# A two-layer transformer block on one core: a new step order for the first feed-forward, grouped bias products, and stack transposes later in an attention slot

## The reference

```python
# layer 0, attention: 16 heads of 16, causal, then a projection
ctx = softmax(mask(Q K^T) / 4) V          # Q, K, V from x @ W.T
x = LN(x + ctx @ Wp.T + bp)
# layer 0, feed-forward: 8 experts, all computed, 2 of them weighted per token
gates = top-2 of softmax(x @ router_w + router_b), renormalised
h = gelu(x @ expert_w[e] + expert_b[e])   # e = 0..7, 256 wide
x = LN(x + (sum_e gates[e] * h[e]) @ out_w + out_b)
```

## Time and profile before

| | |
|---|---|
| median of 3 runs | 989.48 us (987.34 to 991.6) |
| the profiled execution | 989.61 us, span 987.7 us |
| busy share of the span | PE 89%, DVE 73%, ACT 52%, POOL 39% |
| first attention | to about 262 us |
| first feed-forward | to about 453 us, partly overlapped |
| mean granted TensorE clock | 0.965 of full |

### The profile page before, as it was taken

One profiled execution on the slowest core, in us unless ns is written; L12 is line 12 of the kernel. 1 busy time (PEld: TensorE's weight loads), 2 busy tenths in 40 slices (PEclk: granted clock), 3 DMA queues, 4 the chain that ended last, 5 costly groups with the idle time before them and its releaser, 6 DMA issues.

```text
span 987.7 us, 22438 instructions
## 1 busy us (share of the span) xinstructions
PE 875.0 (89%) x8350; PEld 538.7 (55%) x8457; DVE 717.2 (73%) x1955; ACT 513.9 (52%) x1201; POOL 383.7 (39%) x729
## 2 busy tenths in 40 slices
PE   5887878987579888998999999999999999899996
PEld 2444545443234444335555666766666676577654
DVE  3776766676567877657999888888888888733566
ACT  3566657666224343436666665555555555432542
POOL 3543445444334554442333333332333332300185
PEclk8998989999779999999999999999999999999999
DMA  7323322320000000002676766555555666600011
GB/s 261 101 82 81 67 54 66 89 29 7 2 1 1 1 1 1 1 1 41 121 120 117 112 99 103 96 104 97 95 99 103 98 104 95 119 3 1 1 44 43
DMA packets 210428, 65.64 MB, mean 66 GB/s; under 512 B 203008, under 2 KB 206608, under 8 KB 210192
## 3 DMA queue, kind: packets, MB, share of 16 engines
q1 hardware_dynamic: 210320, 64.19, 33.3%
HBM read 17.92 MB, written 4.19 MB: 22 GB/s over the span
## 4 chain that ended last, share of the span: by engine, by line
PE 53%; DVE 21%; issue 7%; POOL 6%; DMA 6%; ACT 6%; SPq 1%; POOLq 0%; DVEq 0%; ACTq 0%
PE bank L417 12%; PE bank L418 11%; PE bank L416 10%; DMA att<-w_lo 5%; PE bank L760 3%; PE bank L762 3%; PE bank L761 3%; DVE nm L1230 3%; PE bank L543 3%; DVE w_lo L1254 2%; ACT scr L895 2%; DVE scr L1172 2%; ACT att L941 2%; POOL scr L1714 2%; PE bank L464 2%
## 5 line engine op out<-in xcount | busy, mean ns | idle before, releaser
L985 ACT ACTIVATE att<-att,nm 128x512 f32<-128x512 f32 (+3 forms) x256 | 141.5, 553 | 104.1 <-DVE nm L1243 102.7
L416 PE MATMUL bank<-w_hi,scr 128*128 128x256 bf16 (+1 forms) x566 | 169.4, 299 | 6.1 <-DVE scr L1172 3.1
L417 PE MATMUL bank<-w_lo,scr 128*128 128x256 bf16 (+1 forms) x575 | 173.1, 301 | 1.9 <-issue 1.8
L418 PE MATMUL bank<-w_hi,scr 128*128 128x256 bf16 (+1 forms) x572 | 171.9, 301 | 0.1
L895 ACT ACTIVATE scr<-bank 128x256 bf16<-128x256 f32 (+3 forms) x208 | 110.2, 550 | 112.1 <-PE bank L762 43.0
L1230 DVE TENSOR_REDUCE nm<-bank 128x1 f32<-128x512 f32 (+3 forms) x256 | 110.3, 483 | 44.0 <-PE bank L488 44.0
L1243 DVE CUSTOM_DVE_ANT_0 att<-bank,consts 128x512 f32<-128x512 f32 (+3 forms) x256 | 113.4, 483 | 15.0 <-PE bank L418 15.0
L941 ACT ACTIVATE att<-bank 128x512 f32<-128x512 f32 (+1 forms) x192 | 90.9, 528 | 61.3 <-PE bank L527 60.6
L1749 POOL TENSOR_SCALAR wqkv_hi<-att,rr 128x512 bf16<-128x512 f32 (+3 forms) x128 | 66.0, 535 | 140.2 <-DVE rr L1260 140.2
L1172 DVE TENSOR_TENSOR scr<-bank,scr 128x256 bf16<-128x256 f32 (+1 forms) x144 | 75.1, 535 | 48.2 <-ACT scr L895 48.2
L1749 POOL TENSOR_SCALAR w_hi<-att,rr 128x512 bf16<-128x512 f32 (+3 forms) x128 | 66.0, 535 | 104.6 <-DVE rr L1260 104.6
(11 more groups left out here) (177 smaller groups left out, 2107.4 us busy)
## 6 DMA issues: line engine op xcount, KB each, us to landing
scr<-wall_in SPq DMA_DIRECT2D x19, 512.0 KB, 4.7
x_tok<-x_tok_in SPq DMA_DIRECT2D x1, 2048.0 KB, 10.2
v_by_token<-scr SPq DMA_DIRECT2D x16, 128.0 KB, 1.8
scr<-v_by_token SPq DMA_DIRECT2D x16, 128.0 KB, 3.2
scr<-x_t_in SPq DMA_DIRECT2D x3, 512.0 KB, 6.0
out<-x_tok SPq DMA_DIRECT2D x3, 512.0 KB, 2.7
scr<-wqkv_in SPq DMA_DIRECT2D x2, 384.0 KB, 3.4
att<-w_hi SPq DMA_TRANSPOSE x32, 3.3
```

The lines of the kernel that those rows point to most:

```text
L416: pe.matmul(out, l_hi, r_hi, start=start, stop=False, skip_group_check=check)
L417: pe.matmul(out, l_hi, r_lo, start=False, stop=False, skip_group_check=check)
L418: return pe.matmul(out, l_lo, r_hi, start=False, stop=stop, skip_group_check=check)
L985: last = act.activation(at, at, ACT.Exp, bias=nm[:, j % 2, qt:qt + 1], scale=-1.0, accum_out=rs[:, j % 2, qt:qt + 1])
```

## The change

1. `small_weights` runs in slot 18 (`SMALL_SLOT`); the load of the biases stands with the first loads; the pieces are laid out in slot 27 by twelve DMAs, three to each of the partitions 0, 32, 64 and 96, in the place of a used q/k/v weight.
2. The bias products are issued together, for the four pairs of experts, each on its own 32 rows of the array, behind the six products of experts 0.
3. The order of a step changes on all engines, as the diff shows. The join of the two sums moves from the end of step t to step t + 1, cm turn and second product to the end of step t + 1, `joined(t, 2)` and `norm(t, 2)` to step t + 2.
4. In attention, `l0_stack` comes after the context turns (even slots) and after `l0_context(g, 0)` (odd slots).
5. `x_low` of blocks 2 and 3 is POOL's, in slots 7 and 15.

```diff
-TURN_LEADS = (("x1", LEAD), ("x2", -2), ("cm", -1), ("cc", LEAD + 2))
+TURN_LEADS = (("x1", LEAD), ("cc", LEAD + 2), ("cm", -1), ("x2", -2))
 STEPS = range(-LEAD - 2, NT + 2)
 EARLY = range(-LEAD - 2, -2)
 TURNS = [(kind, n + lead) for n in STEPS for kind, lead in TURN_LEADS if 0 <= n + lead < NT]
 DVE_X = 5
-MIX = DVE_X + 1
...
 BIAS_SLOTS = range(27, 31)
+SMALL_SLOT = 18
...
+        eb3 = wqkv_hi[:, 0, 0:512]
...
-        eb3 = scr[0:3, 15360:16384].bitcast(BF16)
...
             sp.dma_start(b1_col[:, :], b1_d).then_inc(ld_b, 16)
+            sp.dma_start(eb_f, eb_d).then_inc(ld_b, 16)
...
-                    sp.wait_ge(ch_done, NCH)
-                    sp.dma_start(eb_f, eb_d).then_inc(ld_b, 16)
-
-            sp.wait_ge(eb_ready, 1)
-            for i in range(3):
-                sp.dma_start(eb3[i:i + 1, :], eb_p[:, i, :]).then_inc(eb_moved, 16)
+                if p == BIAS_SLOTS[0]:
+                    sp.wait_ge(eb_ready, 1)
+                    sp.wait_ge(a["vp"], NT)
+                    for q in range(4):
+                        for i in range(3):
+                            sp.dma_start(eb3[32 * q + i:32 * q + i + 1, :], eb_p[4 * q:4 * q + 4, i, :]
+                                         ).then_inc(eb_moved, 16)
+
...
                     if chunk == 0 and 0 <= p + 1 < NP:
                         l0_row_maxima(p + 1)
+                    if chunk == 1 and j == 0 and 0 <= g - 1 < NT:
+                        l0_context_turns(g - 1)
+                    if chunk == 1 and j == 1 and 0 <= g < NT:
+                        l0_context(g, 0)
                     if chunk == 1 and 0 <= g + 2 < NT:
                         l0_stack(g + 2, j)
-                    if chunk == 1 and j == 0 and 0 <= g - 1 < NT:
-                        l0_context_turns(g - 1)
                     if chunk == 2 and 0 <= g + 3 < NT:
                         (l0_project, l0_values)[j](g + 3)
-                    if chunk >= 1 and j == 1 and 0 <= g < NT:
-                        l0_context(g, chunk - 1)
+                    if chunk == 2 and j == 1 and 0 <= g < NT:
+                        l0_context(g, 1)
                     if (p, chunk) in EARLY_AT:
                         if EARLY_AT[p, chunk] == 0:
                             pe.wait_ge(ch_done, 1)
...
-                hold(pe, m["ge"], 4 * (t - 1) + p + 1)
                 out = bank[4 + p][:, :]
-                pe.matmul(out, ones_b[0:3, :], eb3[:, p * 512:(p + 1) * 512], start=True, stop=False)
+                if p == 0:
+                    hold(pe, m["ge"], 4 * (t - 1) + 1)
                 for k in range(KE):
                     cs = slice(EXPW + k * NX * E + p * 512, EXPW + k * NX * E + (p + 1) * 512)
                     last = mm3(out, tb_hi[t % TB][:, k * P:(k + 1) * P], tb_lo[t % TB][:, k * P:(k + 1) * P],
-                               w_hi[:, cs], w_lo[:, cs], False, k == KE - 1)
+                               w_hi[:, cs], w_lo[:, cs], p == 0 and k == 0, p > 0 and k == KE - 1)
+                if p == 0:
+                    hold(pe, m["ge"], 4 * t)
+                    for q in (1, 2, 3, 0):
+                        rows = slice(32 * q, 32 * q + 3)
+                        last = pe.matmul(bank[4 + q][:, :], ones_b[rows, :], eb3[rows, :], start=(q > 0), stop=(q == 0),
+                                         tile_position=(32 * q, 0))
                 last.then_inc(m["f"], 1)
...
-            pe.wait_ge(eb_moved, 48)
+            pe.wait_ge(eb_moved, 12 * 16)
...
                     l1_project("k", 0)
                 if here:
                     experts(n, 0)
-                if 0 <= n + 4 < NT and (n + 4) % TT == TT - 1:
+                routed = 0 <= n + 4 < NT and (n + 4) % TT == TT - 1
+                if routed:
                     logits((n + 4) // TT)
-                if 0 <= n - 2:
-                    turn_mix("x2", n - 2)
-
-                routed = 0 <= n + 4 < NT and (n + 4) % TT == TT - 1
                 if 0 <= ahead < NT and not routed:
                     first_project(ahead)
                 if here:
                     experts(n, 1)
                 if 0 <= ahead < NT and routed:
                     first_project(ahead)
-                if 0 <= behind < NT:
-                    turn_mix("cm", behind)
                 if 0 <= n + LEAD + 2 < NT:
                     turn_mix("cc", n + LEAD + 2)
...
@@ -713,11 +718,15 @@
                 if here:
                     experts(n, 2)
                 if 0 <= behind < NT:
-                    second_project(behind)
+                    turn_mix("cm", behind)
                 if n == NT:
                     l1_project("v", 0)
                 if here:
                     experts(n, 3)
+                if 0 <= n - 2:
+                    turn_mix("x2", n - 2)
+                if 0 <= behind < NT:
+                    second_project(behind)
             l1_project("q", 0, 1)
...
                     l1_high("k", 0)
                 if here:
                     gelu(n, 0)
+                if 0 <= n + 4 < NT and (n + 4) % TT == TT - 1:
+                    router_exp(m, (n + 4) // TT + 1, TT * NX)
+                if here:
+                    gelu(n, 1)
+                if 0 <= n + LEAD + 2 < NT:
+                    turned_high("cc", n + LEAD + 2)
+                if n == NT:
+                    l1_high("q", 0, 0)
+                if here:
+                    gelu(n, 2)
+                if 0 <= n - 1 < NT:
+                    turned_high("cm", n - 1)
+                if n == NT:
+                    l1_high("v", 0)
+                if here:
+                    gelu(n, 3)
                 if 0 <= n - 2:
                     turned_high("x2", n - 2)
-                if here:
-                    gelu(n, 1)
-                if 0 <= n - 1 < NT:
-                    turned_high("cm", n - 1)
-                if 0 <= n + LEAD + 2 < NT:
-                    turned_high("cc", n + LEAD + 2)
-                if 0 <= n + 4 < NT and (n + 4) % TT == TT - 1:
-                    router_exp(m, (n + 4) // TT + 1, TT * NX)
-                if n == NT:
-                    l1_high("q", 0, 0)
-                    l1_high("v", 0)
-                if here:
-                    gelu(n, 2)
-                    gelu(n, 3)
             l1_high("q", 0, 1)
...
-                if p in X_SLOTS:
+                if p < 0 and p in X_SLOTS:
                     x_low(X_SLOTS[p])
...
-                if 0 <= n - 2:
-                    turned_low("x2", n - 2)
                 if here:
                     mix(n, 0)
+                if 0 <= n - 2:
+                    joined(n - 2, 2)
+                if 0 <= behind < NT:
+                    join_halves(behind)
                 if 0 <= ahead < NT:
                     joined(ahead, 1)
-                if 0 <= behind < NT:
-                    turned_low("cm", behind)
                 if 0 <= n + LEAD + 2 < NT:
                     turned_low("cc", n + LEAD + 2)
                 if n == NT:
                     l1_low("q", 0, 0)
                 if here:
                     mix(n, 1)
+                if 0 <= n - 2:
+                    norm(n - 2, 2)
                 if 0 <= ahead < NT:
                     norm(ahead, 1)
-                if 0 <= behind < NT:
-                    joined(behind, 2)
                 if routed:
                     choose_first((n + 4) // TT)
+                if 0 <= behind < NT:
+                    turned_low("cm", behind)
+                if n == NT:
+                    l1_low("v", 0)
                 if here:
                     mix(n, 2)
+                if routed:
+                    choose_second((n + 4) // TT)
+                    gate((n + 4) // TT)
                 if 0 <= n + LEAD + 3 < NT:
                     context(n + LEAD + 3)
-                if n == NT:
-                    l1_low("v", 0)
-                if 0 <= behind < NT:
-                    norm(behind, 2)
-                if routed:
-                    choose_second((n + 4) // TT)
-                if routed:
-                    gate((n + 4) // TT)
-                if here:
-                    join_halves(n)
+                if 0 <= n - 2:
+                    turned_low("x2", n - 2)
             l1_low("q", 0, 1)
...
+            def x_low(b):
+                pool.wait_ge(x_hi_d, x_pieces(b) + 1)
+                ts = ds(b * TOK, TOK)
+                pool.tensor_tensor(xt_lo[:, :, ts], xt_f[:, b % 2, :].rearrange("p (k t) -> p k t", k=KE),
+                                   xt_hi[:, :, ts], ALU.subtract).then_inc(x_lo_d, 1)
...
+                    x_low(X_SLOTS[p - 1])
                 if p in POOL_HALVES:
                     split_chunk(*POOL_HALVES[p])
                 if p in BIAS_SLOTS:
                     add_bias(p - BIAS_SLOTS[0])
-                if p == BIAS_SLOTS[-1] + 1:
+                if p == SMALL_SLOT:
                     small_weights()
...
-            def norms(n):
```

(41 more changed lines are left out.)

1 line of the change is left out of this document (removed).

## The result

The changed kernel took 963.13 us (median of 5 runs, 958.42 to 963.47), the kernel before 989.48 beside it (987.34 to 992.84): ratio 0.9719, 95% interval 0.9703 to 0.9735. By the ratio that is 27.8 us less, by the two medians 26.3; 962 was predicted. The profiled execution took 958.42, the lowest of the five, against 989.61 before: 31.2 less.

A forecast was written before the change was run, and what follows sets the result against it. TensorE, busy 89% of the span, was taken to bound the kernel, with plain steps a loop through four engines. Terms -10.4 - 1.5 + 0.5 - 5.5 - 8.2 - 2.85 = -27.95 from 989.6 gave 962 us, range 949 to 977.

The forecast's parts named there:

- 1, `x_low` on POOL: Attention: moving `x_low` of blocks 2 and 3 from VectorE to POOL removes two stalls; -10.4 us, bad bound +6.
- 2, stack later: Attention: later stack transposes fill TensorE's waits but delay VectorE's k stack copy; -1.5 us, bounds -5 and +5.
- rival (b): Attention: the k stack's delay lands in the slots; +5 us over the value taken, 967 us; chance 0.15.
- The prediction's own sign of being wrong: Attention: the forecast is wrong if TensorE waits for the k stack's copy in most odd slots; no size given.
- 3, bias pieces: Bias load and layout: the earlier load costs +0.5 us; TensorE's wait between the stages ends, -5.5 us.
- 4, the group: First feed-forward: four bias products together take 0.5 us in place of 1.7; -1.2 us a step.
- (c): First feed-forward: bias group runs in turn or drains; +0.6 to +1.2 us in 16 steps, 973 us; chance 0.13.
- 5, new order: First feed-forward: join moves a step later, VectorE's loop sets plain steps at 9.45 us; step 1 to scores -8.2 us.
- Step 0: First feed-forward's opening step: its last gelu comes sooner, so the first mix of step 1 is 2.85 us earlier.
- (a): First feed-forward: TensorE's 8.6 us sets plain steps; 6 less, up to 3 more, 954 us or less; chance 0.2.
- (d): First feed-forward: second product waits for the end of VectorE's whole list; plain step 13.5 us, total 999; chance 0.04.

The follow-up runs named there:

- e2: The kernel before with only `x_low` of blocks 2 and 3 moved to POOL; 981.05 us, ratio 0.9903 to the kernel before.
- e1: The changed kernel with the old order of the stack transposes in attention; 959.41 us, ratio 0.9688 to the kernel before.
- e3: The kernel before with only the new order of the stack transposes; 994.59 us, ratio 1.0040 to the kernel before.
- e8: The changed kernel with the new stack order in even slots only, the old one in odd slots; 953.87 us, ratio 0.9635 to the kernel before.
- e4: The kernel before with only the bias pieces split and laid out early, in six DMAs; 984.13 us, ratio 0.9938 to the kernel before.
- e6: The kernel before with bias pieces early and bias products grouped, in the old order of steps; 981.73 us, ratio 0.9906 to the kernel before.
- e5: The changed kernel with each bias product again ahead of its own six, new step order kept; 974.06 us, ratio 0.9826 to the kernel before.
- e7: The changed kernel with VectorE's cm low part ahead of the norms and TensorE's second product ahead of the x2 turn; 957.44 us, ratio 0.9666.
- e9: The changed kernel with the edits of e8 and e7 together; 951.65 us, ratio 0.9609 to the kernel before.

## Why the prediction was right, step by step

**Right in total, 962 against 963.13, and this closely by luck: errors of both signs cancel.** The stack order came out 4.5 to 5.5 us worse than its term. The stretch from step 1 to the scores, forecast 8.2 us shorter, was 12.3 shorter in the profile, and 2.1 more came from the part that nobody touched. By the experiments, one part alone:

- **1, `x_low` on POOL:** -10.4 predicted, -9.6 in e2. Right.
- **2, stack later:** -1.5 predicted, +3 to +4 measured (e1, e3). This step failed, and its rival (b) is what happened. The working had both numbers: 5 us of filled waits against up to +9, "+9, less the 5". I then wrote that VectorE "is still at its maxima when the stack ends", so that part of the 0.72 us goes unseen. The rows after say it is not: VectorE stands 8.7 us ahead of these copies. That sum, +4, was the value. The prediction's own sign of being wrong, that TensorE waits for the k stack's copy in most odd slots, is there: 11 stops in twelve of them. e8 and e1 separate the terms: -5.2 for the even slots, +8.3 for the odd ones.
- **3, bias pieces:** -5.5 + 0.5 predicted, -6.1 in e4, and 5.3 less in the trace at the place named. Right.
- **4, the group:** 0.5 assumed, 0.42 measured; (c) fell. But "-1.2 a step" is no property of the group: it was 3.2 in all in the old order and 10.6 in the new (e6, e5), where 1.2 in 16 steps would be 19.
- **5, new order:** the stop of the join went and the new loop closes where I said. Mis-sized terms: a plain step 8.9, not 9.45 (VectorE's part 5.5 and TensorE's 3.4, each a little less), though steps 2 and 6, ahead of routed ones, took 9.5; TensorE's own work 7.8, not 8.6; routed steps 11.85 at full clock and 13.0 at 0.87, not 13.4, which leaned on the 13.7 counted from join to join (12.65 from mix to mix); step 11 took 11.84 at 0.86, not 10.9 (10.19 at full clock in e1); steps 1 to 14 together 128.4, not 133.5. The tail is 17.8, not 16.7: its last product ran at the lower clock and took 1.4 more than in e7. My picture of the old loop, "the last gelu, POOL, the join, the turn", was wrong in its first link: e6, and already the trace before, show VectorE's list down to the statistics of the second norm and POOL's deviation there. It did no harm, since the new order moves that deviation too.
- **Step 0** and all before it: -19.75 predicted to the first mix of step 1, -16.8 in the profile, 3 short. Term 2 explains more than that, 4.5 to 5.5; step 0 itself gave 3.5 for 2.85, and what else went 1 to 2 us the other way isn't shown.

**The rivals.** (a), TensorE alone sets plain steps: no, it stops 1.1 of 8.92; in e5, with 1.26 more work, it is true. (d), the second product waits for VectorE's whole list: no, it starts at 312.78, right after the cm low part, with more of the list to come.

The group and the new order don't simply add. e2, e3 and e4 give -9.6 + 4.0 - 6.1 = -11.7. e5, which has the new order but not the group, stands at -17.2, so the order by itself is worth about 5.5 if the other three parts add. With the group's 3.2 of the old order that makes 8.7, but together they gave 27.8 - 11.7 = 16.1.

**Left open.** Four of the five executions of the changed kernel took 962.7 to 963.5, the profiled one 958.42. Its first slots ran at full clock; whether the others had the late clock of e7's and e9's profiles wasn't seen, as only one execution each is profiled. The clock of the routed steps is open as well. It is step 7 that has the lower one here, but with the same instructions it was step 3 in e8, and both (0.87) in e1. Steps 3 and 7 of e8:
```profile
286.87:300.64 13.77, 10.51 (x51) 5.28 (x50) 11.09 (x40) 5.79 (x11) 5.53 (x10) 0.75 0.00 1
327.98:339.84 11.86, 8.55 (x54) 4.80 (x54) 11.00 (x41) 5.79 (x11) 5.53 (x10) 1.00 0.00 1
```

## What to carry to other kernels

When an edit moves a producer later to fill its engine's wait, ask of each of its uses who reads it next and whether that reader is idle; here the same edit paid 5.2 us in even slots and cost 8.3 in odd ones, and doing it in the even ones alone beats both all and none. The price of an instruction is that of the loop it stands in: the same 1.26 us a step were worth 3.2 us in all in an order bound by two other engines and 10.6 in one where TensorE stands still for only 1.1 us of a step. When an instruction is moved out of a loop, look at what the move puts into it: the x2 turn took back 0.44 of the 0.7 that the norms had given. To learn what closes a loop, read the idle time of each engine in it from the trace, POOL's included, not the order in which the code names them.

## What was not expected of the hardware

- The same subtraction of 128x1024 took 2.99 us on VectorE at 80.99 us, 2.13 on POOL, and 1.22 on VectorE at 22.42 us in the kernel after, with POOL idle beside it. Beside the 2.99 POOL was at an operation of 2.12 us that had begun at 80.78, 0.2 earlier; from its end at 82.90 to VectorE's at 83.98 are 1.1. The Trainium skill (SBUF — State Buffer, section Who interferes with whom) says that a VectorE instruction with two SBUF inputs contends with a GpSimd instruction that reads SBUF, over ports that are locked for one of them, and that the order of issue decides who is blocked. These rows agree: the later one, VectorE's, took longer by about what was left of POOL's. So the edit moved 3 us of VectorE's to 2.1 of POOL's.
- The granted clock differs between executions at one and the same place: 0.69 or 1.00 at 31 to 42 us. With the same attention code, the stack of the last even slot came 2.5 us later for it in e7 (213.83, in the changed kernel 211.31) and 4.1 in e9 (206.18, in e8 202.07).
